# A queue of full expert tiles that runs across images, in place of tiles padded for each image

## The reference

```
gate = softmax(xt @ Wg)                      # xt: layer-normed tokens, 8 experts
topv, topi = top_k(gate, 2); topv = topv / (sum(topv) + 1e-6)
scores = zeros(T, 8); scores[t, topi] = topv
for e in range(8):
    h = gelu(xt @ W1[e] + b1[e])             # 128 -> 512
    out = out + (h @ W2[e] + b2[e]) * scores[:, e:e+1]      # 512 -> 128
```

## Time and profile before

| | |
|---|---|
| median of three runs | 5300.02 us (5293.02 to 5305.19) |
| the profiled execution | 5304.72 us, of which the span of the profile is 5302.9 us |
| PE busy | 4738.9 us (89%) |
| PEld busy | 2629.4 us (50%) |
| DVE busy | 3577.1 us (67%) |
| ACT busy | 2996.8 us (57%) |
| POOL busy | 1023.8 us (19%) |

### The profile page before, as it was taken

The page is one execution under the profiler, slowest core; times in us unless marked ns, Lnnn a source line. Parts: engine busy times, 40 slices in busy tenths (PEclk is TensorE's granted clock), DMA queues, the critical chain, the costliest instruction groups (busy, mean ns, idle before and its releaser), DMA issues.

```text
span 5302.9 us, 81731 instructions
## 1 busy us (share of the span) xinstructions
PE 4738.9 (89%) x25633; PEld 2629.4 (50%) x25633; DVE 3577.1 (67%) x7651; ACT 2996.8 (57%) x5516; POOL 1023.8 (19%) x1349
## 2 busy tenths in 40 slices
PE   6999999999999969588888888888999999999999
PEld 1222222222222223367777878777655555555554
DVE  6788888888888636556565655655577667667765
ACT  2666667676676724145555555557655554554552
POOL 2222223222232212023333333333100000000000
PEclk7999999999999989689999999999999999999999
DMA  2622223322233112235454554544211111111112
GB/s 61 166 78 69 73 66 98 84 66 77 66 92 83 49 31 28 68 111 169 135 169 138 154 152 145 162 132 134 64 49 52 45 48 51 47 47 51 49 45 76
DMA packets 396856, 461.35 MB, mean 87 GB/s; under 512 B 86136, under 2 KB 248144, under 8 KB 394320
## 3 DMA queue, kind: packets, MB, share of 16 engines
q1 hardware_dynamic: 362688, 409.11, 26.7%
q0 software_dynamic: 20576, 35.55, 2.4%
q10 hardware_dynamic: 13168, 11.48, 0.8%
HBM read 309.59 MB, written 129.84 MB: 83 GB/s over the span
## 4 chain that ended last, share of the span: by engine, by line
PE 34%; DVE 16%; issue 4%; DVEq 4%; ACT 2%; ACTq 0%; SPq 0%; DMA 0%
PE n_ps_f L2212 4%; PE n_ps_f L2205 4%; PE n_ps_xy L1860 4%; PE n_ps_h L1850 3%; PE n_ps_c L2252 3%; PE n_ps_h L2264 2%; PE n_ps_f L2199 2%; PE n_ps_f L1708 2%; DVEq L2084 1%; PE n_ps_xy L2268 1%; PE n_ps_f L1054 1%; DVE n_stats L1030 1%; PE n_ps_h L2268 1%; DVE n_xln L1042 1%; DVE n_down_weights L2083 1%
## 5 line engine op out<-in xcount | busy, mean ns | idle before, releaser
L664 ACT ACTIVATE a_probs<-ps_b 128x512 f32<-128x512 f32 x2048 | 1111.3, 595 | 558.7 <-PE ps_b L748 535.6
L496 DVE TENSOR_REDUCE a_negmax<-ps_a 128x1 f32<-128x1024 f32 x1024 | 1214.5, 1220 | 242.3 <-PE ps_a L696 213.0
L1663 ACT ACTIVATE n_hidden<-n_ps_h,n_b 128x128 f32<-128x128 f32 x1472 | 419.1, 373 | 346.9 <-PE n_ps_h L1850 346.1
L760 PE MATMUL ps_o<-a_probs,a_v_ones 128*32 128x512 f32 x4096 | 547.6, 607 | 0.5 <-ACT a_probs L664 0.5
L1860 PE MATMUL n_ps_xy<-n_down_weights,n_hidden 128*128 x2944 | 411.9, 284 | 79.2 <-ACT n_xy L1677 73.3
L696 PE MATMUL ps_a<-a_k_stack,a_q_stack 96*128 96x512 bf16 x1408 | 404.0, 394 | 58.5 <-DMA a_k_stack<-split_scratch 27.5
L748 PE MATMUL ps_b<-a_q_stack,a_k_stack 99*128 99x512 bf16 x1408 | 442.3, 386 | 14.8 <-ACT a_probs L664 11.9
L1860 PEld LDWEIGHTS n_ps_xy<-n_down_weights,n_hidden 128*128 128x128 f32 x2944 | 370.7, 196 | 117.3 <-issue 113.2
L2149 ACT ACTIVATE n_down_weights<-n_ps_h 128x512 f32<-128x512 f32 x288 | 172.2, 598 | 427.1 <-PE n_ps_h L2264 319.1
L1850 PE MATMUL n_ps_h<-n_xy,n_up_weights 128*128 128x128 f32 x2944 | 403.2, 281 | 3.2 <-issue 1.5
L1368 POOL DMA_INDIRECT rows_scratch<-n_xln,n_index_out x256 | 257.1, 1004 | 666.8 <-DVE n_index_out L1521 563.2
(11 more groups left out here) (349 smaller groups left out, 8154.3 us busy)
## 6 DMA issues: line engine op xcount, KB each, us to landing
n_up_weights<-in_L_ffn_W_dram SPq DMA_DIRECT2D x368, 256.0 KB
n_up_weights<-score_scratch SPq DMA_DIRECT2D x512, 128.0 KB, 2.9
split_scratch<-a_pieces SPq DMA_DIRECT2D x128, 256.0 KB
rows_scratch<-n_zero SPq DMA_DIRECT2D x16, 1472.0 KB, 9.6
outs_scratch<-n_xy SPq DMA_DIRECT2D x176, 128.0 KB
...
```

The source lines that it names most:

```text
L496: dve.tensor_reduce(negmax[:, b, t:t + 1], bank, axis=AX.X, op=ALU.max, negate=True).then_inc(ring_read, 1)
L664: act.activation(probs[:, m % PROBS, 512 * k:512 * k + 512], ps_b[:, k, :], ACT.Exp).then_inc(b_exp, 1)
L760: last = pe.matmul(ps_o[32 * j:32 * j + 32, 512 * k:512 * k + 512], v_ones[:, t, J * g + j, :], probs[:, (J * quad + j) % PROBS, 512 * k:5 ...
L1663: last = act.activation(hidden[:, j % 2, f, :], ps_h[j % 2][:, 128 * f:128 * f + 128], ACT.Gelu, bias=b1[:, bass.ds(e, 1), f:f + 1].rearra ...
```

## The change

Rows of an expert run on across images. Each expert keeps one open tile of 128 rows; when a tile is full it enters a queue and gets a number, and the next image goes on in the tile that is left open. The queue is closed twice (`FLUSHES`), after image 2 and after image 15; unfilled rows of open tiles are then filled with zeros by eight more indirect DMAs. There are 16 x 16 + 14 = 270 tiles, not 368. `begun` gives the tiles at which each stage starts: stage 0 gets 4 tiles, stage 1 14, stage 2 24, each of the stages 3 to 14 16, and stage 15 36. A stage still has 46 slots; `steps_of` spreads its tiles evenly over them, and a stage begins six tiles before the first that its image's routing made sure (`AHEAD`).

For this `routing` computes more: open tiles, what is left in them, tile numbers (`code`), and the queue's owners over a window of 30 places. It has 64 DVE instructions where it had 26 (12 more where the queue is closed), nine of them on 1 x 30 x 8 elements. They are due in slots 23 to 30, not 23 to 33. Rows and results lie in two shared buffers, read and written tile by tile at a number that SP loads from SBUF; the fills of whole buffers with zeros are gone.

Results of images 0 to 2 are gathered and summed in stages 5 to 7. Those of images 3 to 15 can be gathered only when the whole queue is done, so 13 sums, not one, fall into stage three, one beside each of its first 13 images. Lastly the ranking of `gate_choose_steps` in stage three is done in two halves of four token tiles, which halves two buffers.

```diff
+EARLY_IMAGES = 3
+EARLY_TILES = 2 * N * EARLY_IMAGES // 128 + 7
 def gate_choose_steps(dve, t, E, K, eps, tie):
...
+    tiles = t["above"].shape[1] // E
+    for lo in range(0, NT, tiles):
+        shape = (128, tiles, E, E)
...
+        dve.tensor_tensor(above, other, own, ALU.is_gt)
+        yield dve.tensor_tensor(same, other, own, ALU.is_equal)
...
-        TILES = (N * K + E * 127) // 128
+        PER_IMAGE = N * K // 128
+        FLUSHES = (EARLY_IMAGES - 1, B - 1)
+        TILES = PER_IMAGE * B + 2 * (E - 1)
+        WINDOW = 2 * PER_IMAGE - 2
+        AHEAD = 6
+        GATHER_AFTER = 5
+        SLOTS = 46
+        sure = [0] + [PER_IMAGE * (i + 1) - (8 if i + 1 < EARLY_IMAGES else 0) for i in range(B - 1)] + [TILES]
+        begun = [0] + [sure[i] - AHEAD + (2 if i == 1 else 0) for i in range(1, B)] + [TILES]
...
+        def steps_of(i, slot):
+            steps = 2 * (begun[i + 1] - begun[i])
+            return range(2 * begun[i] + steps * slot // SLOTS, 2 * begun[i] + steps * (slot + 1) // SLOTS)
...
-            def clear(i):
-                sp.dma_start(x_dram[i][:, :]...., zero[...]).then_inc(zeroed, 16)
+            def load_rows(q):
+                if q >= 4:
+                    sp.wait_ge(x_ps, q - 3)
+                i = routing_of[2 * q]
+                if 2 * q == sure[i]:
+                    sp.wait_ge(S["owner_up"], i + 1)
+                    sp.wait_ge(scattered, scattered_by(i + 1))
+                for n in range(2):
+                    c = code_of(2 * q + n)
+                    sp.dma_start(xg[:, q % 4, n, :], tiles_of(x_dram, 2 * q + n)[bass.ds(c, 1), :, :]....).then_inc(x_in[q % 4], 16)
+            def store_pair(q):
+                sp.wait_ge(moved, q + 3)
+                for n in range(2):
+                    c = code_of(2 * q + n)
+                    sp.dma_start(tiles_of(y_dram, 2 * q + n)[bass.ds(c, 1), :, :]...., xy[...]).then_inc(y_stored[q % 2], 16)
...
+                if i in FLUSHES:
+                    for e in range(E):
+                        gp.indirect_dma_start(rows_of(x_dram, i), bass.IndirectOffsetOnAxis(index_pad[:, e:e + 1], 0), zero[:, :], None).then_inc(scattered, 16)
+            for i in range(B):
+                scatter(i)
+                if 0 <= i - GATHER_AFTER < EARLY_IMAGES:
+                    gather(i - GATHER_AFTER)
+            for i in range(EARLY_IMAGES, B):
+                gather(i)
...
             def routing(i):
+                dve.tensor_tensor(need[:, :], left[:, :], counts[:, NT, :], ALU.add)
+                dve.scalar_tensor_tensor(limit[:, :], has[:, :], 128.0, left[:, :], ALU.mult, ALU.subtract)
...
+                window = (1, WINDOW, E)
+                yield dve.tensor_tensor(marked[:, :, :], places, by_expert(first), ALU.is_equal)
+                dve.tensor_tensor(entered[:, :, :], places, by_expert(first), ALU.is_ge)
...
                 for n, _ in enumerate(routing(i)):
                     if n % 2:
-                        yield 23 + n // 2
+                        yield 23 + n // 3
...
             def experts(i, stages):
-                side_by_side(stages + ([combine(i - 1)] if started(i) else []))
+                side_by_side(stages + ([combine(i - GATHER_AFTER)] if 0 <= i - GATHER_AFTER < EARLY_IMAGES else []))
...
-            run_dense(combine(B - 1))
+            run_dense(lambda i: combine(i + EARLY_IMAGES) if i + EARLY_IMAGES < B else None)
...
     def pipeline(engine, attention, choice, experts, beside=None):
         for i in range(0, B - 2):
-            experts_and_stages(i, [choice(i + 1, True), attention(i + 2)] + (list(beside) if i == 0 else []))
+            more = beside(i) if beside else None
+            experts_and_stages(i, [choice(i + 1, True), attention(i + 2)] + ([more] if more else []))
```

427 lines of the change are left out of this document (254 added, 173 removed).

## The result

The changed kernel takes 5462.5 us (median of 4 runs, 5456.5 to 5466.7) against 5299.0 of the kernel before on the same chip: 1.031 times, 95% interval 1.029 to 1.0325. Slower, as forecast, but by 163 us and not by 51. It lies above the range (5272 to 5405).

A forecast was written before the change was run, and what follows sets the result against it. It took each stage as one chain through PE, DVE and ACT: DVE sets the opening, PE the closing. Terms +3.7 - 8.6 + 3 + 4 - 4 + 2 + 27 + 24 = +51 us on 5300, called 5350; range 5272 to 5405.

The forecast's parts named there:

- Newton part: Third part of a stage, holding routing: 24.4 us of DVE work plus about 2 of waits, 26.4 us, +4.6.
- The rival that DVE's waits take it in: Newton steps: DVE's waits absorb the added routing, the part stays at about 21 us, total 5274; chance 0.17.
- PE busy under 60%: Sign that the forecast is right: in the Newton part of stages 3 to 13, PE is busy under 60%.
- Opening: Slots 0 to 14 of an ordinary stage, set by DVE: 0.8 us less, bounds 0 and 2.
- Closing: Last 11 slots of an ordinary stage, bound by PE: 2.6 us less, bounds 1.5 and 7.2.
- such a fall only as a rival: PE idles more and its clock falls: 1.7 us a stage, 24 us in 14 stages, total 5374; chance 0.14.
- Second part: 8 to 9 slots between opening and Newton steps: 1.6 us less, bounds 0 and 2.4.
- Lead-in and stages 0 to 2: Routing of image 0 in the lead-in +3.7 us, stage 0 -8.6, stage 1 +3, stage 2 +4.
- Stages 14 and 15: Stage 14 +2 us, bounds -8 and +8, for more routing; stage 15 +27 us for its 36 tiles.
- The halves: Stage three's ranking in halves, running count three slots later, one before PE needs it: 0 us, bounds -10 and +10.
- A sum: Each later sum in stage three costs 2.0 us; twelve more make 24 us, bounds 0 and 66.
- PE busy 236 us less: Over the span, 98 tiles fewer take some 236 us off PE's busy time.

The follow-up runs named there:

- e5: The kernel before with 38 more 8-element DVE instructions, each with its drain, spread over routing in slots 23 to 30: 5417 us.
- e7: The changed kernel with ACT's expert step of slot 7 behind the token-row copy, and stage three's ranking steps two slots apart, not three: 5448 us.
- e4: The changed kernel with eleven spare PE products in each chain of Newton steps, into columns nothing reads: 5449 us.
- e1: The kernel before with only stage three's expert ranking done in two halves of four tiles: 5328 us.
- e2: The changed kernel without the gathers and weighted sums of images 3 to 15: 5423 us.
- e11: The changed kernel with routing behind the scatter's signal, except weights, on POOL, sums earlier, ACT's slot-7 step later, stage three ranking in one piece: 5385 us.

## Why the prediction was wrong in size

The direction was right, the places were not: the forecast had +53 us in stages 14, 15 and three and -4 in stages 3 to 13, which lost 58.5. The miss of 110 us (161.5 for 51) is 63 in stages 3 to 13 (opening 41, closing 26, Newton part 10, second part -14), 44 in stage three and 4 elsewhere.

- **Newton part: right.** 26.4 us forecast, 27.3 measured, DVE without waits until the last copy. In stage 5 that is 27.9 less a wait of 3.6, so 24.3 us of DVE's work for 24.4, although the trace has 66 instructions of routing and eleven over 240 elements where the forecast counted 64 and nine. Its sign "PE busy under 60%" failed: 21.1 of 27.9 us, 76%, at a clock of 0.68 that the forecast did not expect. e5 shows the count of instructions as the cause, also with 23 tiles. The rival that DVE's waits take it in is refuted.
- **Opening: the step that failed first.** "I allow 0.8 us for one `move` less in front of ACT's copy", bounds 0 and 2: measured +2.9, 41 us in eleven stages beside the forecast. I counted the steps that fall away and not where the remaining ones land. With 16 tiles a GELU falls into slot 7 ahead of the copy (2.3 us, e7), and PE's gap before the transposes grows to 6.8 us and they run at half clock (0.9 us longer; that this is the rest of the loss is argued, not shown). The lengths with 23 tiles and with none did not bound it: what counts is where the steps fall.
- **Closing: mis-sized by the clock.** 2.6 us less forecast, 0.2 less measured (20.2 to 20.0 in the mean): 26 us beside the forecast. It is 16.3 to 16.9 in three stages, in which the mechanism was right, 18.7 in two, and 22.0 to 22.5 in six, with a long fall of the clock. The prediction had such a fall only as a rival, at 1.7 us a stage from one gap; a fall can take 27.3 us at 0.50 and cost 5. e4 shows that the clock makes the long closings; why a fall is long in one stage and short in another stays open.
- **Second part:** -1.6 forecast, -2.9 measured, beyond the bound of 2.4, which came from a stretch at a clock of 0.78.
- **Lead-in and stages 0 to 2:** +3.7, -8.6, +3, +4 forecast, +6.8, -2.7, +2.0, +5.2 measured, and -4.4 in what comes before them. Stage 0 has the longer Newton part (28.6 us) and closing (17.5) too.
- **Stages 14 and 15:** +29 forecast, +28 measured (-2 and +30 for +2 and +27).
- **Stage three: two terms mis-sized.** The halves stood at 0, bounds -10 and +10; they cost 25 us (e1). The prediction saw that the count would stand one slot ahead of PE's need and gave that no price. A sum stood at 2.0 us, read from one image; it costs 3.5 in that place (e2), so 42 and not 24. One image with and one without was too little: it compares two images that differ in more than the sum.
- **PE busy 236 us less: wrong.** 33. Expert work fell by 174, and PE's other products took 141 more. Most of that is the clock, as far as the mean clocks tell: some 380 us of stages 3 to 13 at half clock, for 80.
- The queues of SP were hidden as forecast. The rows never came late in the changed kernel, but did in e11.
